# Gathered-row loads of a mixture-of-experts stage issued by SyncE instead of ScalarE

## The reference

```python
x = x + tanh(g_xattn[0]) * xattn(layernorm(x), ctx_512, ...)   # 16 heads, 375 context rows
x = x + tanh(g_ffn[0])   * ffn(layernorm(x), ...)

def ffn(h, ...):                        # h: 1792 tokens x 512
    logits = h @ gate_w.T               # 64 experts
    topv, topi = top_k(logits, 8)
    W = scatter(softmax(topv))          # a weight for each of a token's 8 experts
    gate, up = split(einsum('nh,eih->nei', h, gu_w))      # 128 each
    out = einsum('nei,ehi->nh', silu(gate) * up * W, dp_w)
    return out + sigmoid(h @ sh_gate1_w.T) * shared_expert(h)
```

## Time and profile before

| | |
|---|---|
| time, median of 3 runs | 1608.14 us (1606.47 to 1611.97) |
| the profiled execution | time 1608.14 us, span 1606.3 us |
| TensorE | busy 1436.9 us, 89% of the span |
| VectorE | busy 1138.8 us, 71% |
| ScalarE | busy 673.2 us, 42% |
| GpSimd | busy 782.0 us, 49% |
| moved by DMA | 380.08 MB, mean 237 GB/s |

### The profile page before, as it was taken

The page is one execution under the profiler, slowest core; times in us unless marked ns, Lnnn a source line. Parts: engine busy times, 40 slices in busy tenths (PEclk is TensorE's granted clock), DMA queues, the critical chain, the costliest instruction groups (busy, mean ns, idle before and its releaser), DMA issues.

```text
span 1606.3 us, 24946 instructions
## 1 busy us (share of the span) xinstructions
PE 1436.9 (89%) x7674; PEld 1171.9 (73%) x7674; DVE 1138.8 (71%) x2601; ACT 673.2 (42%) x1558; POOL 782.0 (49%) x858
## 2 busy tenths in 40 slices
PE   7999799999799989989999989987399989998985
PEld 5766677787588767768777768865398979888742
DVE  5777674198778248888627888625488889988687
ACT  3333574011277101158401117512177767776521
POOL 4654573055477727667334777425334333333322
PEclk9999899999999999999999999998599999999998
DMA  7897992555595866720185753165899999999698
GB/s 242 298 318 266 293 289 79 188 174 184 184 288 170 277 225 221 222 76 17 36 287 172 237 187 128 42 230 176 250 322 328 346 346 357 366 339 329 209 425 344
DMA packets 164358, 380.08 MB, mean 237 GB/s; under 512 B 20200, under 2 KB 55682, under 8 KB 162434
## 3 DMA queue, kind: packets, MB, share of 16 engines
q1 hardware_dynamic: 135622, 283.20, 52.7%
q0 software_dynamic: 20608, 62.28, 11.3%
q10 hardware_dynamic: 7996, 33.01, 6.5%
HBM read 238.82 MB, written 139.59 MB: 236 GB/s over the span
## 4 chain that ended last, share of the span: by engine, by line
PE 57%; DMA 17%; DVE 13%; issue 5%; POOL 4%; ACT 2%; SPq 1%; ACTq 0%; POOLq 0%; DVEq 0%
PE bank L737 15%; PE bank L738 14%; PE bank L739 14%; DMA w_ex<-in_w_ex 7%; PE bank L835 6%; DMA p_in<-parts 3%; DMA kv_raw<-in_ctx 3%; PE bank L861 3%; DVE q_sin L1150 2%; PE bank L1000 1%; POOL slot_rows L1841 1%; POOL q_rope L1819 1%; DVE q_rope L1146 1%; POOL prob L1825 1%; DMA wq_s1l<-wq_dram 1%
## 5 line engine op out<-in xcount | busy, mean ns | idle before, releaser
L1819 POOL TENSOR_TENSOR q_rope<-q_rope,q_sin 128x448 f32<-128x448 f32 x192 | 218.0, 1164 | 173.2 <-DVE q_sin L1150 173.1
L1897 POOL DMA_INDIRECT parts<-y_sb,to_row x140 | 135.7, 970 | 240.8 <-ACT y_sb L1725 214.0
L1825 POOL TENSOR_TENSOR prob<-prob,row_inv 128x375 f32<-128x375 f32 x219 | 176.8, 814 | 100.5 <-DVE row_inv L1172 99.0
L835 PE MATMUL bank<-q_rope,m_w 128*128 128x448 f32 x384 | 156.4, 543 | 12.3 <-DVE q_tl L1156 9.1
L1150 DVE TENSOR_TENSOR q_sin<-bank,sin_q 128x448 f32<-128x448 f32 (+1 forms) x256 | 158.3, 618 | 3.9
L1164 DVE TENSOR_REDUCE row_max<-bank 128x1 f32<-128x375 f32 x224 | 119.7, 535 | 43.0 <-PE bank L739 42.4
L1841 POOL DMA_INDIRECT slot_rows<-rows,pos_i x112 | 109.5, 977 | 74.6 <-DVE count L1257 46.5
L861 PE MATMUL bank<-ident,prob 128*125 128x128 f32 x672 | 115.2, 282 | 33.0 <-POOL prob L1825 22.2
L861 PEld LDWEIGHTS bank<-ident,prob 128*125 128x125 f32 x672 | 103.1, 190 | 43.3 <-POOL prob L1825 32.9
L1574 ACT ACTIVATE prob<-bank,row_max 128x375 f32<-128x375 f32 x224 | 128.4, 573 | 9.9 <-DVE row_max L1164 9.4
L835 PEld LDWEIGHTS bank<-q_rope,m_w 128*128 128x128 f32 x384 | 70.7, 189 | 67.5 <-issue 64.0
(11 more groups left out here) (360 smaller groups left out, 4400.8 us busy)
## 6 DMA issues: line engine op xcount, KB each, us to landing
w_ex<-in_w_ex SPq DMA_DIRECT2D x64, 768.0 KB, 10.7
slot_rows<-blank SPq DMA_DIRECT2D x64, 612.0 KB
p_in<-parts SPq DMA_DIRECT2D x14, 2048.0 KB, 16.8
m_w<-m_dram SPq DMA_DIRECT2D x48, 192.0 KB, 2.4
x_g<-slot_rows ACTq DMA_DIRECT2D x16, 476.0 KB
x_g<-slot_rows ACTq DMA_DIRECT2D x12, 612.0 KB
wq_s0h<-wq_dram SPq DMA_DIRECT2D x24, 256.0 KB, 3.5
wq_s0l<-wq_dram SPq DMA_DIRECT2D x24, 256.0 KB, 3.9
```

Of the source, the lines that this page charges most:

```text
L835: m = pe.matmul(bank[5][:, 0:GT], m_w[n % NW][:, c, :], q_rope[h % 2][:, c, :], start=(c == 0), stop=(c == QC - 1))
L1819: pool.tensor_tensor(o[:, c, :], o[:, c, :], q_sin[:, c, :], ALU.add).then_inc(s_radd, 1)
L1825: pool.tensor_tensor(prob[i][:], prob[i][:], row_inv[:, i:i + 1].to_broadcast([P, L]), ALU.mult)\
L1897: pool.indirect_dma_start(parts, bass.IndirectOffsetOnAxis(ap=to_row[x % NROW][0:size, t:t + 1], axis=0), y_sb[x % NY][t][0:size, :], None)\
```

## The change

`load_slots` moves from ScalarE to SP, with its waits, its register load and its transfer. ScalarE keeps one wait, for the routing of the last batch. SP issues the first five right after `wait_attention_over`, ahead of `spare`, and in its loop each further one stands ahead of `load_expert`: at place x first `load_slots(x + 5)`, then `load_expert(x + 3)`. On ScalarE it stood in turn x behind `inner(x)`.

```diff
@@ sync(sp)
+            def load_slots(x):
+                e = sp.value_load(order[0:1, x:x + 1], min_val=0, max_val=E - 1)
+                size, n = TILES[x]
+                if x >= NXE:
+                    sp.wait_ge(s_et, FIRST[x - NXE + 1])
+                    sp.wait_ge(s_own, 3 * (x - NXE) + 1)
+                sp.dma_start(x_g[x % NXE][0:size, 0:n, :], slot_rows.rearrange("(e m) w -> e m w", m=SPAN)
+                             [bass.ds(e, 1), 0:size * n, :].rearrange("one (p t) w -> p (one t) w", t=n))\
+                    .then_inc(s_xg[x % NXE], 16)
+
             for step, b in END:
                 finish(step, b)
             sp.wait_ge(s_order, 1)
             for x in range(NE):
                 load_expert(x)
             wait_attention_over(sp)
+            for x in range(NXE):
+                load_slots(x)
             sp.dma_start(spare[:], a["c_spare"]).then_inc(s_spare, 16)
             for x in range(E):
+                if x + NXE < E:
+                    load_slots(x + NXE)
                 if x + NE < E:
                     load_expert(x + NE)
                 if x in REST_AT:
@@ scalar(act)
             for step, b in END:
                 finish(step, b)
-            act.wait_ge(s_order, 1)
-            wait_attention_over(act)
-
-            def load_slots(x):
...
-            for x in range(NXE):
-                load_slots(x)
+            act.wait_ge(s_route, NR * B)
@@
                     split_expert(x + 1)
                 if x < E:
                     inner(x)
-                if x + NXE < E:
-                    load_slots(x + NXE)
                 if x >= 1:
                     down(x - 1)
```

## The result

The changed kernel is slower: 1633.14 us in the median of four runs (1631.64 to 1637.74) against 1607.63 us (1606.47 to 1611.97), a ratio of 1.0158 with a 95% interval of 1.0131 to 1.0186.

What follows compares the result with a forecast made beforehand. TensorE was taken to bound the first twelve experts, DMA those from 1268 us. A 5.6 us later start plus 1.8 us of slow clock gave 7.4 us on 1608.1: 1615.5 us, range 1607.0 to 1618.5.

Steps and rivals of the forecast that it cites:

- The late `spare`: Start of expert stage: `spare` lands behind five `x_g` loads, moving TensorE's first product of expert 1 by 5.6 us; chance 0.74.
- The clock: After TensorE's near-idle stretch at the stage start, half clock speed costs 1.8 us (0 to 2.3).
- The first part: Stage start: expert 0's split no longer waits behind ScalarE's `x_g` issues; gain 0.5 us, at most 0.9, not subtracted.
- The order of the loads: Through the expert stage: each later `x_g` goes out one period earlier, ahead of `w_ex`; cost 0 us.
- The failed step: Later DMA-bound experts: the same bytes move from a later start, so the initial 7.4 us is neither regained nor enlarged.
- the steady issue: Later `x_g` loads in the expert loop: earlier issue, same bytes, extra transfer absorbed while TensorE sets the pace; 0 us.
- The forecast of about 24 us of `w_ex` waits: Expert stage: waits for `w_ex` stay about 24 us; clearly less or more would show the prediction wrong.
- rows 7: Profile before, transfers by queue at the stage start: read as service in order of issue, even across queues.
- Nothing late: Rival, stage start: `spare` overtakes the `x_g` bytes or finishes early, leaving only the 0.5 us gain; 1607.6 us, chance 0.11.
- SP late: Rival, expert loop: SP issues each `w_ex` 0.5 us late, 21 times, adding 10.5 us; 1626.0 us, chance 0.05.
- Faster: Rival, DMA-bound experts: early `x_g` and the single queue thin out `w_ex` stalls; 1603.6 us with half gone, chance 0.05.
- Turns between the queues: Rival: DMA alternates between SP's and ScalarE's queues, so one queue relieves `w_ex` once by 1.8 us; 1613.7 us, chance 0.05.

Runs made afterwards that it cites:

- e1: Changed kernel with `spare` loaded ahead of the first five `x_g` loads; 1635.20 us against 1614.55 for the kernel before, ratio 1.0164.
- e4: Kernel before, with the `spare` load taken from SP and put behind ScalarE's first five `x_g` loads; 1626.63 us, ratio 1.0054.
- e11: Changed kernel, `spare` still behind the five `x_g` loads, with two-tile `x_g` loads on 128 partitions; 1597.85 us, ratio 0.9888.
- e9: Changed kernel with `spare` first, all `x_g` on SP, and two-tile `x_g` loads on 128 partitions; 1589.29 us, ratio 0.9848.
- e8: Kernel before, on its two queues, with two-tile `x_g` loads on all 128 partitions; 1589.37 us against 1614.04, ratio 0.9836.
- e10: e8 with expert 0's weights split ahead of ScalarE's first five `x_g` loads; 1594.48 us, ratio 0.9872 to the kernel before.
- e2: Kernel before, with each later `x_g` load issued one expert earlier, still by ScalarE; 1613.11 us against 1614.55, ratio 0.9982.
- e3: e1 with each later `x_g` load issued on SP one expert later, the old order in one queue; 1642.49 us, ratio 1.0179.
- m1: Program of transfers alone in 16 phases, varying partitions and queues, no kernel time; weight and 112-partition loads: 268 GB/s on one queue, 310 on two.
- e5: Queues swapped: `x_g` on SP with `spare` first, later `w_ex` on ScalarE; 1606.45 us against 1605.79 for the kernel before, ratio 0.9999.
- e7: Kernel before, with the 28 `xs` and `base` loads moved from SP to ScalarE's queue; 1606.63 us, ratio 1.0008.
- e6: Kernel before, with the odd `x_g` loads from number 5 on issued by SP in the old order; 1614.90 us, ratio 1.0068.

## Why the prediction was wrong

The sign and the first mechanism were right, the size was not; the forecast stopped at less than a third of the loss.

*The late `spare`: right.* Predicted was a first product of expert 1 that is 5.6 us later (4.6 to 6.7), measured 4.98. The clock was to cost 1.8 us (0 to 2.3): it is 0.50 from 1177.50 to 1182.00, and the records get shorter at 1182.21, so 4.7 us at half speed, 2.3 us. Together 7.3, seen 7.1, predicted 7.4: that the sum fits so well is luck in part, as the first product came 0.6 us less late than forecast and the clock cost 0.5 more. `w_ex` 3 is issued 16.4 us behind the first `x_g`; predicted was 17.1. e1 takes the stall away, e4 and e11 make it alone.

*The first part: as taken.* TensorE starts 4.90 us behind the first issue, 4.65 before; expert 1's transposes start 7.28 us behind it instead of 8.07, so 0.8 us earlier, and the wait for `spare` swallows it, as forecast. Only e9, with `spare` first, reaches expert 3 0.8 us earlier than its partner e8, and e10 shows that the same early split costs 5 us once SP is free to issue `w_ex` 3.

*The order of the loads: right at 0 us* with two queues, by e2. In one queue the late order of e3 costs more than the early one of e1, by 5.5 us.

*The failed step.* It is "in the DMA regime the same bytes have to move from a start that is later by the same amount", and with it "Its bytes are the same" as the reason for costing the steady issue at 0. The bytes were the same, the rate was not: 62.92 MB at 351 GB/s are 179 us, 63.19 MB at 319 are 198. I read the DMA share of 1.02 as a full DMA and its rate as fixed. But 351 GB/s is less than weight loads reach alone (395), and the share was 1.02 at 319, 351 and 408 GB/s alike. The forecast of about 24 us of `w_ex` waits, with clearly more as a sign of being wrong, fell with it: they were 46.2. The trace of before had it on record: 3.13 MB of `x_g` alone, at about 91% of the engines' time, took 14 us, which is 224 GB/s. I timed `spare` by such a rate and did not ask what such a load does to its neighbours.

*What the runs put in its place.* Loads of `x_g`'s kind on 96 or 112 partitions are slow alone (248 and 266 GB/s against 382 on 128; 104 and 120, which the kernel has too, weren't timed alone). Beside weight loads they slow the whole, and in one queue more than in two: 268 against 310 GB/s in m1. In the kernel it is 319 or 320 where `x_g` and `w_ex` share a queue (after, e1, e3), 351 to 356 where they don't (before, e2, e4, e5, e7), and 332 with half of the loads (e6). That step, costed at 0, is the 19.4 us between experts 21 and 53. Take away the few partitions, and one queue or two are equal (e8, e9).

*The rivals.* Nothing late: refuted by the 9.7 us of `spare`. SP late: refuted by the 0.17 to 0.21 us between buffer and issue. Faster: the waits for `w_ex` went from 23.8 to 46.2 us. Turns between the queues: this was the rival closest to the cause, as it let the two streams act on each other, and its sign was wrong. I asked what `w_ex` loses to an `x_g` on the other queue, and not what the two lose in the same one.

The reading of rows 7 as a service in order of issue holds in part. In e8 `w_ex` 3 was issued at 1164.22, and ScalarE's queue, with the five `x_g` issued earlier, went on to have all of the engines' time from 1164.5 to 1168.5 (first line). In e10 `w_ex` 3 was issued only 0.1 us behind `x_g` 0, and from 1156 to 1160 both queues moved (the other two):

```profile
q10 hardware_dynamic: 177, 0.96, 104.5%
...
q1 hardware_dynamic: 117, 0.66, 54.1%
q10 hardware_dynamic: 97, 0.54, 43.0%
```

The Trainium skill's rule of a round robin over the queue rows (DMA: Bandwidth & Descriptors, section Queues, rings and completion order) agrees with e10's stretch, not with e8's and not with 1156 to 1161 in rows 7; what decides between them is open. The other section of the Trainium skill that I cited, Issuing engines are not separate DMA queues, says that issuing from several engines saves only the time to issue; here it holds for 128-partition loads (e8 and e9 are equal) and fails for the mix with 112 partitions (m1's 268 against 310, and e3 against before).

*What stays open.* Why fewer partitions are slow is not shown, nor why the mix in one queue is slower than the two kinds in turn. m1 shows no gain of a second queue beside GpSimd's writes, while the kernel, which has such writes, shows one. Their share of the bytes is alike (15.48 of 62.92 MB before, 5.5 of 20.7 MB in m1), so that isn't the difference. In m1 the loads of a phase don't wait for one another, in the kernel they wait for buffers; whether that matters wasn't tried. So the kernel's own loss rests on the kernels (before, e1, e3, e8, e9), not on m1. And the clock's part of the first loss wasn't tried by itself.

## What to carry to other kernels

A DMA share of 1 is no proof that the rate is fixed: compare the GB/s of the stage with that of its loads alone. If a kind of load is slow, repair its shape first (here one line that loads all 128 partitions and some unused rows, 1.6% faster), since here the choice of queue stopped mattering then. Before loads are moved to another engine's queue, look for the small load that comes behind them and for who waits for it, and put it first. And ask of each buffer that is freed earlier which transfer it lets go, and whose bytes that one runs beside.

## What was unexpected of the hardware

- The number of partitions of a load sets its rate, with packets of the same size: 248 GB/s on 96, 266 on 112, 382 on 128; 487 KB on 112 partitions take 1.83 us at that rate, 557 KB on 128 take 1.46.
- One queue that mixes 128-partition and 112-partition loads runs at 268 GB/s, below the 334 of the two in turn. The same on two queues gives 310, and 5.5 MB of writes beside the one queue are free. The weights' own packets take 347 ns in that mix and 236 alone.
- The DMA share stayed at 1.02 while the rate was 319, 351 or 408 GB/s.
- A load of 5 KB behind five of 612 KB landed after 9.7 us instead of 1.5, and in e4 after 12.1.
- With a weight load issued 0.1 us after the first `x_g`, on another queue, TensorE started 10.0 us behind the issue instead of 4.8.
